# A fused attention and feed-forward layer on Trainium2: the loads at the seam between its first two stages are reordered and their waits narrowed

## What is computed

```python
h = layernorm(x)
q, k, v = split(h @ Wqkv + bqkv)              # 1024 -> 3 x 1024
a = (q @ k.T) / sqrt(1024) * mask              # decay mask inside 128-blocks, 1 elsewhere
x = x + (softmax(a) @ v) @ Wproj + bproj       # one head, all 2048 keys, no causal cut
g, u = h2 @ (wg/127).T, h2 @ (wu/127).T        # h2 = layernorm(x), 1024 -> 3072
x = x + (silu(g) * u) @ (wd/127).T
```

## Time and profile before

| | us |
|---|---|
| median of 3 runs | 6050.54 |
| those runs, lowest and highest | 5902.76, 6195.44 |
| the profiled execution's own time | 5522.34 |
| its span (first to last instruction, core 7) | 5520.8 |
| spans of the 8 cores in it | 5487.6 to 5520.8 |

### The profile page before, as it was taken

How to read it: one execution, slowest core, us unless ns; L and a number is a source line. 1 busy time by engine, 2 the same in 40 slices (tenths; PEclk the granted TensorE clock), 3 DMA queues, 4 the chain that set the end, 5 groups by cost and what they waited for, 6 DMA issues and landing times.

```text
span 5520.8 us, 54551 instructions; the slowest of 8 cores (5487.6 to 5520.8 us)
## 1 busy us (share of the span) xinstructions
PE 4955.2 (90%) x22794; PEld 2304.7 (42%) x22794; DVE 1023.7 (19%) x1281; ACT 698.2 (13%) x1056; POOL 83.6 (2%) x123
## 2 busy tenths in 40 slices
PE   2899999983999899998999895999999999999999
PEld 1434444441444444444444442444444444444444
DVE  3222222210111211112111211212121111111111
ACT  2111111110001100011001111101010111111110
POOL 0110000000000000000000000000000000000000
PEclk9989999996999999999999997999999999999999
DMA  4662221116000100411000014211212121212121
GB/s 152 100 93 65 67 65 65 46 62 182 23 24 23 35 23 23 124 45 35 23 24 23 23 31 107 65 63 60 69 59 68 58 73 51 76 54 73 50 71 37
DMA packets 264248, 332.81 MB, mean 60 GB/s; under 512 B 129348, under 2 KB 170308, under 8 KB 262982
## 3 DMA queue, kind: packets, MB, share of 16 engines
q1 hardware_dynamic: 153126, 203.48, 12.5%
q0 software_dynamic: 63776, 58.73, 5.3%
q10 hardware_dynamic: 47104, 67.12, 3.4%
HBM read 260.06 MB, written 100.66 MB: 65 GB/s over the span
## 4 chain that ended last, share of the span: by engine, by line
PE 86%; DMA 7%; DVE 3%; issue 2%; ACT 1%; DVEq 0%; SPq 0%; ACTq 0%; POOLq 0%
PE ps L220 40%; PE ps L739 13%; PE ps L1020 12%; PE ps L648 12%; PE ps L797 6%; PE ps L699 1%; DMA x1A<-x_scr 1%; DMA k_hi<-k_scr 1%; DVE x1t L808 1%; DVE x1t L804 1%; PE ps L355 1%; DMA wubuf<-wu_scr 1%; DMA q_scr<-qf_hi 1%; DMA q_scr<-qf_lo 1%; DMA wtmp<-wqkv 1%
## 5 line engine op out<-in xcount | busy, mean ns | idle before, releaser
L648 PE MATMUL ps<-k_hi,qt_hl 128*128 128x512 bf16 x2048 | 469.6, 380 | 100.1 <-DMA qt_hl<-q_scr 100.1
L220 PE MATMUL ps<-xn2f_hi,wgbuf 128*128 128x512 bf16 x1536 | 374.6, 388 | 70.5 <-DMA wubuf<-wu_scr 70.5
L1020 PE MATMUL ps<-wd_sb,hf_hi 128*128 128x512 bf16 x1536 | 350.2, 390 | 20.8 <-DVE hf_lo L984 20.8
L220 PE MATMUL ps<-xn2f_lo,wgbuf 128*128 128x512 bf16 x1536 | 364.9, 381 | 0.0
L220 PE MATMUL ps<-xn2f_hi,wubuf 128*128 128x512 bf16 x1536 | 362.9, 379 | 0.0
L220 PE MATMUL ps<-xn2f_lo,wubuf 128*128 128x512 bf16 x1536 | 362.8, 379 | 0.0
L648 PEld LDWEIGHTS ps<-k_hi,qt_hl 128*128 128x128 bf16 x2048 | 200.6, 98 | 343.0 <-issue 102.2
L1020 PE MATMUL ps<-wd_sb,hf_lo 128*128 128x512 bf16 x1536 | 336.7, 379 | 0.0
L739 PE MATMUL ps<-v_hi,at_hi 128*128 128x512 bf16 x1024 | 324.6, 400 | 0.0
L739 PE MATMUL ps<-v_lo,at_hi 128*128 128x512 bf16 x1024 | 320.1, 396 | 0.0
L739 PE MATMUL ps<-v_hi,at_lo 128*128 128x512 bf16 x1024 | 312.7, 388 | 0.0
(11 more groups left out here) (113 smaller groups left out, 3875.9 us busy)
## 6 DMA issues: line engine op xcount, KB each, us to landing
wgbuf<-wg_scr SPq DMA_DIRECT2D x192, 256.0 KB, 2.6
wubuf<-wu_scr SPq DMA_DIRECT2D x192, 256.0 KB, 2.9
xsA<-x SPq DMA_DIRECT2D x32, 512.0 KB, 3.8
qt_hl<-q_scr SPq DMA_DIRECT2D x32, 512.0 KB, 7.7
xres<-x SPq DMA_DIRECT2D x32, 512.0 KB, 4.9
x_scr<-x1t POOLq DMA_DIRECT2D x32, 512.0 KB, 7.0
x1A<-x_scr SPq DMA_DIRECT2D x32, 512.0 KB, 4.7
y<-outA ACTq DMA_DIRECT2D x32, 512.0 KB, 4.8
```

The lines of the kernel that those rows point to most:

```text
L220: e.matmul(psum_ap, l, r, start=st, stop=sp),
L648: kb=kb, st=first, sp=last: e.matmul(ps0[:, kb * 512:kb * 512 + KW], lhs, kx[:, dc * S + kb * KW: dc * S + (kb + 1) * KW], start=st, stop=sp),
L1020: e.matmul(psd[:, half * 512:(half + 1) * 512], lhs, wd_sb[:, hc * D + half * 512: hc * D + (half + 1) * 512], start=st, stop=sp),
```

## The change

Four things change, all at the seam between stages A and B.

1. `qt_hl` moves to offset 0 of stage B's arena, on top of `wq_hi`; `k_hi` and all that follow move up by 4 KB per partition. Two unused names go.
2. The last q store and the last k store of stage A get semaphores of their own (`s_st2` for the two of q, `s_st3` for the two of k), so they no longer wait for the v store before them, nor the first k store for q's.
3. `prefetch_q(0)` is issued first, and waits for stage A's last matmul and the q of sequence 0. `emit_k(0)` and `emit_v(0)` follow, and `wp_hi` and `wp_lo` come behind them; `wp_hi` no longer waits for the last store of q.
4. The wait for all of `endA` is replaced by narrower ones: the first score matmul waits for the evacuations of q and k, the first exponential and the first `at_hi` wait for the last store of k, and the first product with v waits for the evacuations of v.

```diff
@@ arena of stage B @@
+        qt_hl, o = at("qt_hl", 2 * D, BF16, o)
+        qt_hi = qt_hl[:, 0:D]
+        qt_lo = qt_hl[:, D:2 * D]
         k_hi, o = at("k_hi", DC * S, BF16, o)
...
         wp_lo, o = at("wp_lo", DC * D, BF16, o)
-        qt_hl, o = at("qt_hl", 2 * D, BF16, o)
-        qt_hi = qt_hl[:, 0:D]
-        qt_lo = qt_hl[:, D:2 * D]
@@ stores of q and k in stage A @@
+                sem = ("s_st" if st != NST - 1 else
+                       ("s_st2" if nm == "q" else "s_st3"))
...
-                           waits=evs, inc="s_st", dma=True)
+                           waits=evs, inc=sem, dma=True)
@@ prefetch_q @@
-            gq = [t_scmm.get(g - 1)] + ([t_qst_final] if g == 0 else [])
+            gq = ([t_scmm.get(g - 1)] +
+                  ([t_lastAmm, t_qst_s0] if g == 0 else []))
@@ emit_scores, emit_softmax, the copy to at_hi, the product with v @@
-                                 (endA if g == 0 else []))
+                                 (t_evqk_last if g == 0 else []))
...
-                (endA if g == 0 else []),
+                ([t_kst_final] if g == 0 else []),
...
-                    waits=[tr] + (endA if g == 0 else []),
+                    waits=[tr] + ([t_kst_final] if g == 0 else []),
...
-                                 (endA if g == 0 else []))
+                                 (t_evv if g == 0 else []))
@@ the seam @@
+        prefetch_q(0)
         emit_k(0, [t_lastAmm, t_kst_s0])
         emit_v(0, [t_lastAmm, t_vst_s0])
-        prefetch_q(0)
+        t_wp = []
+        for (dst, l, eng, sem, gw) in (
+                (wp_hi, 0, "sync", "s_lw", [t_lastAmm]),
+                (wp_lo, 1, "gpsimd", "g_lw", [t_lastAmm, t_qst_final])):
+            t_wp.append(P(eng, lambda e, dst=dst, l=l: e.dma_start(
...
+                waits=gw + [("g_wps", plan.cnt["g_wps"])],
+                inc=sem, dma=True))
         prefetch_x(0)
```

More of the change, by code:

```diff
@@ L185, in build_program @@
         x1t, o = at("x1t", D, F32, o)
-        wptmp, _ = at("wptmp", D, F32, starts["qt_hl"])
-        wptmp2, _ = at("wptmp2b", D, F32, starts["a32"])
         b_end = o
@@ L542, in build_program @@
                 t_kst_s0 = t_store["k"]
+                t_qst_s0 = t_store["q"]
                 t_vst_s0 = t_vst[(st, NSUB - 1)]
@@ L546, in build_program @@
         t_qst_final = t_store["q"]
[L547 to L557, removed]
+        t_kst_final = t_store["k"]
+        t_evqk_last = list(t_evqk_prev.values())
+        endA = plan.now("s_st", "s_st2", "s_st3", "te", "ve", "sc",
+                        "s_lx", "s_lw")
         t_exp = {}
@@ L682, in build_program @@
         t_s2done = [None]
+        prefetch_q(0)
         emit_k(0, [t_lastAmm, t_kst_s0])
         emit_v(0, [t_lastAmm, t_vst_s0])
-        prefetch_q(0)
+        t_wp = []
[3 more added lines that the diff above has]
+            t_wp.append(P(eng, lambda e, dst=dst, l=l: e.dma_start(
+                out=dst.rearrange("p (c d) -> p c d", c=DC),
+                in_=wp_scr[l].rearrange("c p d -> p c d")),
+                waits=gw + [("g_wps", plan.cnt["g_wps"])],
+                inc=sem, dma=True))
         prefetch_x(0)
```

## The result

| | us |
|---|---|
| before, median of 12 runs (5502.02 to 6195.44) | 5529.0 |
| changed, median of 10 runs (5460.51 to 6415.33) | 5512.0 |
| ratio of the undisturbed runs | 0.9905, 95% interval 0.9868 to 0.9943 |
| forecast | 5990, range 5800 to 6150 |
| forecast of the sum for the profiled execution | 5462 |

A forecast was written before the change was run, and what follows sets the result against it. TensorE was taken to bound the kernel, with 100.10 us idle at the seam from load traffic and order; starting tile 1's scores at 1325 instead of 1385.30 us gains 60, taken off the 6050.54 median: 5990 us, range 5800 to 6150.

The forecast's parts named there:

- the sum: Whole kernel: tile 1's scores start at 1325 instead of 1385.30 us, 60 us gained, bounds 46 to 74; profiled execution 5462 us.
- The rival of a gap twice as long: Runs without a profile: TensorE's idle time is 1.93 times as long, gain 116 us, 5935 us; chance 0.12.
- the signs that were to refute the forecast: Among them: the span behind tile 1's scores grows, or the gap's 60 us show in the trace and not the median.
- its worst: Seam with `qt_hl` last again: only the 15.5 us of the earlier start are gained, 6035 us.
- Start: First score matmul at the seam: starts at 1246 us (1244 to 1248), about 17 us behind stage A's last matmul.
- Score blocks: Tile 0's scores: blocks 2 to 4 wait 10.5 us per `k_hi` piece; scores end at 1283 to 1288 us.
- The product with v: First product with v: done at 1317 to 1322 us, its v pairs of 7.69 us each arriving just in time.
- What is late next: Before tile 1's scores: 27.3e6 bytes at 286 GB/s take 95.3 us, so TensorE waits 3 to 8 us for `qt_hl`.
- Costed at nothing: Stage A's store semaphores, last k store before the exponential, `wp_hi`, `wp_lo` and `xres`: none was to cost TensorE time.
- The clock gave nothing back: Behind the seam: TensorE's granted clock falls, 37.5 us per 1%; 6103 us at 3% less; chance 0.10.
- the one of faster loads: Seam loads: 345 GB/s stands and v pairs set the pace, gain 79 us, 5971 us; chance 0.10.
- the one of slow small runs: Seam loads: `qt_hl`'s small runs wait, traffic at 230 GB/s, gain 37 us, 6013 us; chance 0.13.

## Why the prediction was wrong, and where it was right

**Where it failed.** The failed step is the one behind the sum: "I take the 60 us off their median: 5990 us". The sum itself gave 5462 us for an execution like the profiled one, and four of the ten runs took 5460.51, 5467.16, 5467.77 and 5478.77 us. The text had both numbers, and left the right one out of the range. The rows spoke for it: the sum was made of them, and nothing in them explained 528 us.

What the runs showed in its place: hundreds of us come and go with the granted clock on part of the chip, with the kernel unchanged. The runs that went with the experiments list the cores of 15 more executions of the kernel before. Six took 5508 to 5518 us, with all cores at 0.958 to 0.961; the other nine took 5583 to 6478, and in each at least four cores had 0.947 or less. (Of the first three runs themselves only the times are on record, so for them it is inferred.) The median of a few runs is thus decided by how many of them fall on such an execution, and so in part is the measured 5512.0 us. The rival of a gap twice as long falls too: on the disturbed cores of the changed kernel's profile, which took some 180 us longer, the seam was 101.6 and 102.3 us, only 6 longer.

That 5462 was met so closely is in part luck. It started from an execution whose slowest core had a clock of 0.954 and ended stage A 20 us or more later than cores 0 to 5 did, and in each of the four runs that met it two or four cores had 0.959 to 0.961. One more execution of the changed kernel, with all cores at 0.965 or 0.966, took 5445.44 us.

**Its own signs.** Two of the signs that were to refute the forecast came up, and neither decides. The gap's gain shows in the trace and hardly in the plain medians (17 us), for the reason just given; it shows in the ratio of the undisturbed runs. The span behind the seam grew by 4 us, within its scatter.

**What bounds the kernel.** Right: the wait was a matter of traffic and its order. The change without the narrowed waits keeps 43 of the 59 us, without the q tile in front 23; the prediction had put this last case, its worst, at 15.5.

**Start.** The first score matmul was put 17 us behind stage A's end and came at 12.6 to 15.1.

**Score blocks.** The forecast of 54 to 59 us for their end was nearly met with 56.4 to 59.8, by two errors that partly cancel. The pieces took 10.5 us each in the sum; the blocks started 12.4 us apart on average (13.8, 9.5 and 14.6 on core 3), with stores and then `v_hi` under way beside them. That costs 6 us over three pieces, and the start that came 2 to 4 us sooner gave about half of it back. The stops did cost the full clock: the first eight matmuls of each block took 3.1 to 3.5 us instead of 1.89.

**The product with v.** Put at 88 to 93 us behind stage A's end, it ended at 89.6 to 93.1, and its v came in time but for 1.2 us on core 2. "That just holds" was right.

**What is late next.** Right in kind and size: tile 1's `qt_hl` was late by 3.7 to 5.3 us (3 to 8 forecast), behind `wp_hi`, and moving `wp_hi` took the wait away. The traffic count gave 95.3 us from the first issue, the seam has 96.0. What the count left out is that the issue of `xres` would be held for 8.56 us behind `wp_hi`; the prediction had put `xres` at nothing.

**Costed at nothing.** Right for the changed kernel: the exponential started 10 us behind the last k store's landing (7 to 12 forecast). But the semaphores hold that cover up, and without them 4.6 us are lost. The step took the value of an edit from the kernel in which it was made and not from the one in which it is missing.

**The sum.** 60 us forecast, 59 at the seam, 54 in the mean span of cores 0 to 5, 52 by the ratio (31 to 73 by its interval). The clock gave nothing back: cores 0 to 5 had 0.959 to 0.961 before and 0.964 to 0.966 now, as it must when 59 us of idling at 0.50 drop out of 5440 (0.5 x 59 / 5440 = 0.005). That rival falls, and so does the one of faster loads: 282 GB/s, and 312 at best with everything under way at once. So does the one of slow small runs, which had 230 GB/s and tile 1's scores at 119 us.

## What to carry to other kernels

When a stage begins with a long wait for loads, list what its first instruction needs and issue that first; then count the bytes in front of each next consumer in its own queue, since the wait moves there. More DMAs under way at once are not faster when the engines are already nine tenths busy: a chain that holds back what is needed later protects what is needed now. And when a few timed runs lie well above the profiled execution, and far apart, forecast the gain from the profile and take more runs before trusting their level.

## What the runs showed of the hardware

DMAs of several queues share the engines, and what lies beside a transfer sets its time more than its size does: the same 1 MB store of q took 4.5 us alone, 5.8 to 10.7 on core 3 beside the chained loads (change 5.8, v held back 8.7, one store semaphore 10.7), and 28.0 with all loads under way. The fourth `k_hi` piece took 9.3 us without `v_hi` beside it and 14.6 with it (issued at 1248.6, its block started at 1263.21). The small runs of `qt_hl` did not starve: `qt_hl` and the first `k_hi` piece, 1.5 MB, landed within 15 us of their issue in spite of two other queues. And an issue can itself take long: that of `xres` held SP for 8.56 us behind `wp_hi` and for 0.35 us without it.
